# The found indices turned and copied directly behind the gathers, ahead of the projections and their evacuation

## The reference

```python
sim = jnp.where(jnp.arange(Tn) <= i, k @ q_i, -jnp.inf)
_, top_idx = jax.lax.top_k(sim, M)               # M = 8 keys out of at most 256
idx = jnp.concatenate([jnp.full((nc, 1), i), top_idx[slots]], axis=1)
K = k[idx]; V = v[idx]                            # subsets of 2 and of 3 keys
det = jnp.linalg.det(jnp.einsum('cnd,cmd->cnm', K, K))
score = log(where(valid, det, 1.0) + 1e-06) / (s + 1)
out_s = softmax(K @ q_i / 4) @ V                  # per subset
y = softmax(scores) @ outs
```

## Time and profile before

| what | value |
|---|---|
| median of 3 runs | 6865.02 us (6857.94 to 6873.23) |
| profiled execution | 6853.56 us |
| its span | 6851.9 us |
| PE busy in the span | 4985.4 us (73%) |
| DVE busy | 4293.3 us (63%) |
| POOL busy | 3267.7 us (48%) |
| ACT busy | 2061.2 us (30%) |
| mean granted TensorE clock | 0.731 |

### The profile page before, as it was taken

One profiled execution on the slowest core, in us unless ns is written; L12 is line 12 of the kernel. 1 busy time (PEld: TensorE's weight loads), 2 busy tenths in 40 slices (PEclk: granted clock), 3 DMA queues, 4 the chain that ended last, 5 costly groups with the idle time before them and its releaser, 6 DMA issues. The chain is left out here.

```text
span 6851.9 us, 140450 instructions
## 1 busy us (share of the span) xinstructions
PE 4985.4 (73%) x45364; PEld 3654.2 (53%) x45365; DVE 4293.3 (63%) x9002; ACT 2061.2 (30%) x6098; POOL 3267.7 (48%) x4341
## 2 busy tenths in 40 slices
PE   5777776987878888888888888334971997169990
PEld 2333333775555555555555555333850776069990
DVE  5777776227889989999899999723654333212223
ACT  3343333223333333333333333221210332123330
POOL 1222222115667777777777777334235000554447
PEclk8676777997666666666666666557985996589995
DMA  4000000002222222222222222212222002111113
GB/s 140 7 5 5 7 3 6 0 4 73 74 73 75 75 73 76 73 76 75 75 76 73 76 76 74 57 37 72 76 72 60 0 0 61 56 50 45 46 43 110
DMA packets 170739, 369.46 MB, mean 54 GB/s; under 512 B 35650, under 2 KB 100939, under 8 KB 169140
## 3 DMA queue, kind: packets, MB, share of 16 engines
q1 hardware_dynamic: 136404, 283.77, 12.6%
q0 software_dynamic: 33792, 78.69, 3.6%
HBM read 286.86 MB, written 75.50 MB: 53 GB/s over the span
## 5 line engine op out<-in xcount | busy, mean ns | idle before, releaser
L2333 POOL TENSOR_TENSOR l2a_prod<-l2a_keys 128x64 f32<-128x64 f32 (+1 forms) x2304 | 1143.7, 528 | 626.9 <-ACT l2a_norms L2224 619.7
L2678 PE MATMUL l2a_g<-l2a_feat,l2a_onehot 128*128 128x33 bf16 x27648 | 828.3, 187 | 49.4 <-DVE l2a_onehot L2544 24.8
L2678 PEld LDWEIGHTS l2a_g<-l2a_feat,l2a_onehot 128*128 128x128 bf16 x27648 | 807.2, 103 | 57.5 <-DVE l2a_onehot L2544 32.3
L2647 PE MATMUL l2a_s<-l2a_qkT 32*128 32x128 f32 (+1 forms) x1536 | 612.9, 489 | 53.3 <-issue 53.2
L2544 DVE TENSOR_SCALAR l2a_onehot<-l2a_spread,l2a_key_col 128x2048 bf16<-128x2048 bf16 x576 | 545.7, 974 | 141.4 <-DMA l2a_spread<-index_rows 105.1
L1734 POOL TENSOR_TENSOR l_hc<-l_hs,l_bc 128x512 f32<-128x512 f32 x192 | 243.1, 1266 | 794.2 <-DVE l_hs L1808 790.7
L2553 DVE TENSOR_REDUCE l2a_dots<-l2a_prod 128x72 f32<-128x1152 f32 x384 | 515.7, 1343 | 54.2 <-POOL l2a_prod L2339 54.2
L1903 PE MATMUL l_y<-l_hc,l_selT 128*96 128x512 f32 x384 | 308.2, 897 | 294.0 <-POOL l_hc L1734 294.0
L2596 PE MATMUL l2a_a<-l2a_tT,l2a_wqk 96*96 96x256 f32 x1024 | 408.9, 570 | 124.5 <-ACT l2a_tT L2175 124.5
L2222 ACT COPY l2a_keys<-l2a_g 128x128 f32<-128x128 f32 x768 | 199.7, 260 | 816.5 <-PE l2a_g L2678 800.5
L440 POOL DMA_INDIRECT rows_in<-l3f_dispatch_xn,l3f_dispatch_at x128 | 122.9, 960 | 652.5 <-ACT l3f_dispatch_xn L416 613.8
(11 more groups left out here) (403 smaller groups left out, 10979.3 us busy)
## 6 DMA issues: line engine op xcount, KB each, us to landing
l2a_spread<-index_rows SPq DMA_DIRECT2D x384, 512.0 KB, 3.7
rows_in<-main_zeros SPq DMA_DIRECT2D x1, 13824.0 KB, 59.4
l2f_xg<-rows_in SPq DMA_DIRECT2D x72, 192.0 KB, 2.4
rows_out<-l2f_ys POOLq DMA_DIRECT2D x72, 192.0 KB, 2.4
l3f_xg<-rows_in SPq DMA_DIRECT2D x72, 192.0 KB, 2.4
rows_out<-l3f_ys POOLq DMA_DIRECT2D x72, 192.0 KB, 2.4
l3f_w<-in_l3f_w SPq DMA_DIRECT2D x2, 4608.0 KB, 33.9
l_xT<-in_l_xT SPq DMA_DIRECT2D x16, 384.0 KB, 3.8
```

Source lines behind the costliest of these rows:

```text
L2333: nc.gpsimd.tensor_tensor(made[:, j, at:at + wide * wide, :].rearrange("p (b a) f -> p b a f", b=wide), key[:, lo:lo + wide, :].unsqueeze( ...
L2647: nc.tensor.matmul(o, qkT[rows, u, h // 3, t * P:(t + 1) * P], qkT[rows, u, 4 + h // 3, 0:nk], start=True, stop=False, skip_group_check=True)
L2678: ins = nc.tensor.matmul(g_ps[j][:, a * FEAT:(a + 1) * FEAT], onehot[:, s[2] % 2, kt, j * SLOTS + a, :], feat3[:, s[1], kt, piece, h, :], ...
```

## The change

On ACT `copy_turned` moves from the end of the body to the place right behind `cast_index`, ahead of the stage functions, `normalise` and the evacuation of `front`. On PE `turn_index` moves from the end of the body to the place right behind the gathers, ahead of `turn_output` and `front`. All instructions, waits and buffers stay the same.

```diff
@@ ACT
                     if real:
                         cast_index(n, u, i)
+                        copy_turned(n, u, i)
                     for k, do in ((SIMS, differences), (DENOM, denominators), (GAP, gaps), (DET, logs),
                                   (SCORE, weights), (OUT, out)):
...
                     if i == 0 and real:
                         split_middle(n, u)
-                    if real:
-                        copy_turned(n, u, i)
@@ PE
                     if s3:
                         gather(s3, 0)
                         gather(s3, 1)
+                    if not (isinstance(n, int) and n == B):
+                        turn_index(n, u, i)
                     if previous(n, u, i, OUT):
                         turn_output(*previous(n, u, i, OUT))
                     nxt = next_image(n, u, last)
                     if nxt and FRONT <= i < FRONT + 8:
                         front(*nxt, i - FRONT)
-                    if not (isinstance(n, int) and n == B):
-                        turn_index(n, u, i)
```

## The result

The changed kernel takes **7087.14 us** (median of 4 runs, 7079.75 to 7122.75), the kernel before 6863.94 (4 runs, 6857.94 to 6873.23). The ratio is 1.0334 with an interval of [1.0298, 1.0371]: 3.3% slower, where +22 us and a range up to 6960 had been forecast. The profiled execution took 7079.75 us, its span 7078.1 against 6851.9, its mean granted clock 0.694 against 0.731.

The account below looks back on a forecast made before the run. DVE was taken as the bound at 90% busy, PE close behind at 82%. A PE loss of 88 us less a gain of 66 us gave +22 us on 6865, so 6887 us, range 6805 to 6960.

Parts of the forecast that it names:

- The spread waits go: DVE's one-hot comparison (L2544): its waits for the spread indices, 105.1 us, nearly vanish, to under 20 us.
- The gain of 66 us: DVE in steps 2 and 3: earlier indices save 2.13 us per image, limited by POOL's product, over 31 images.
- ACT's wait for PE, costed at nothing: ACT's early copy waits for PE's turn, 0.6 us per step with the copy, covered by later waits for DVE.
- The order on PE, 74 us: PE, steps 3 to 10: turn ahead of front work delays the gather of step 11, 2.4 us per image over 31.
- The clock, 14 us: PE's granted clock: added pauses cost a quarter of one front's 1.76 us, 0.44 us per image.
- Rival 3: PE's clock: one to two more fronts per image at the low level, 80 us more, 6967 us; chance 0.15.
- What would show it: Signs in the changed profile's attention stage: waits, PE pauses, step 11's gather 2 to 4 us later, DVE busy 2507 us.

Follow-up runs that it names:

- e3: Kernel before with the copy of the turned indices early on ACT only in steps 11, 0, 1 and 2, PE unchanged: 6829.19 us, ratio 0.9945.
- e1: Kernel before with only ACT's part, the copy directly behind the cast in all steps, PE unchanged: 6864.91 us, ratio 0.9992.
- e5: e3 plus eight small unread matmuls behind the gathers in every step, the turn still last: 6792.23 us, ratio 0.9879.
- e11: e4 again with more runs, the changed kernel with eight small matmuls ahead of each turn: 6873.96 us, ratio 1.0009.
- e4: Changed kernel with eight small unread matmuls ahead of each turn: 6889.65 us in one run, 1.0036 of the kernel before.
- e6: e4 with four small matmuls before every turn in place of eight: 6997.48 us in one run, ratio 1.0174.
- e9: Kernel before with eight small unread matmuls behind the gathers in every step, nothing else: 6812.4 us, ratio 0.9917.

## Why the prediction was wrong

The sign was right; the size was not (+223 us by the medians, against +22), and the true value lies beyond the range. Step by step:

- **The spread waits go.** Right: 105.1 to 11.0 us. The copy starts 0.47 us after its cast's end in the mean, 1.15 us at most.
- **The gain of 66 us.** Too large: 38 us (e3). What failed there is "POOL's product, issued at 2795.52 and 0.74 us long": the duration is that of a product with no one-hot beside it. With about 1.15 us in both steps the 1.88 us become 1.88 − 0.8 = 1.1 us, and 31 images make 34 us; from the mean of 2.13 us it is 41 us. e3 gave 38. The one-hots show the same: a pair takes 4.62 us beside POOL's weighing (2945.59 and 2946.09, above) and 1.39 us where POOL idles (2964.49). The weighing ends at 2949.67 and the pair 0.54 us later, at 2950.21. So it goes throughout: in the changed kernel's trace 329 of the 576 one-hots start while a POOL instruction runs, and each ends at least 0.547 us after that instruction does, 0.55 in the median, though one alone takes 0.74 us in all. In these rows one engine stands while the other works. The Trainium skill ("SBUF — State Buffer", "Who interferes with whom") has GpSimd and DVE share a port pair that one of them holds for its whole instruction while the other is blocked; these rows agree. This is read from traces, and no run took the two engines apart.
- **ACT's wait for PE, costed at nothing.** Not refuted for the changed kernel: with the turn early ACT waits 0.44 us before its copy. With the turn late it is dear: e1 is 36 us above e3. In steps 3 to 10 the two edits belong together, or neither.
- **The order on PE, 74 us.** The mechanism holds, and the size is near at a high clock: 89 us (e5 to e11). Part of that is luck. Measured as in the last point below, the gather of step 11 ends 4.2 us later in e11 than in e5 (59.3 against 55.1 us), where the sum had 2.4; only 2.9 us per image, 89 over 31, reached the time. The pause of 0.69 us stands before the turn in steps 6 to 11, front behind it, as foretold. The claim that there is little cover was sound for most of it: the waits of L2552 rose well past 100 us.
- **The clock, 14 us.** This is the step that failed and that made the error: "I take a quarter of one front, 0.44 us, per image". By the experiments it is about 178 us, 5.7 us per image, or more than three fronts' worth of 1.76 us. Two things were wrong in it. It priced only the front, while all of PE's work hangs on the level: the scores grew by 102 us, the projections L2595 by 63 us, all of PE by 240 us over the span (5225.6 against 4985.4) with the same 45364 instructions. And it took the long waits for what lowers the level and counted their shortening in the change's favour. The long wait of the projections did vanish (124.5 to 0.7 us), PE's idle time in pauses over 2 us fell from 323 to 234 us, its whole idle time did not grow, and the level still fell. That added matmuls bring it back is a run's result (e4, e6, e11). That the many short pauses are what lowered it fits the rows, but is argued: e6 has less idle time of PE in the stage than e11 (370 us against 420) and as few pauses over 0.5 us (142 against 166), and its level is 0.63, not 0.76. And in the kernel before PE worked 16 us without a pause at 0.50. What sets the level stays open. The Trainium skill ("TensorE: Matmul & The Clock Gate", Part 1) has the throttled clock as the default that activity releases. The runs agree: by that rule eight useless matmuls per step should speed up even the unchanged kernel, and e9 did by 0.8%. How far one single pause moves the level was not tried.
- **Rival 3** had the mechanism, with +80 us on top of the forecast. It was given 0.15 because the longest idle times get shorter, the same misjudgement.
- **What would show it.** The gather of step 11 was to end 2 to 4 us later against DVE's step 3; from the end of L2427 to the end of that gather it is 64.6 us in the image above (2913.55 to 2978.14), and over 31 images, worked out in the same way, 64.6 us in the mean against 56.8 before: 7.7 us. DVE's busy time, forecast unchanged at 2507, is 2599; of these 92 us 58 are one-hots, which stood more behind long POOL instructions (52 took over 1.5 us before, 113 us in all; 61 after, 181 us). The level moved by 0.08, beyond the 0.03 that the text named as proof against it.

## What to carry to other kernels

In a queue that runs in order, a short wait moved ahead of independent work costs its round trip in every step, and on a nearly full PE it can cost more through the clock than through the wait: here about 178 us against 89. Price a change in PE's pauses over all of PE's work at both levels, not over the instructions next to the pause. The sum of the idle time did not show the danger here; the number of pauses did, though it did not predict the level of e6. If one product must be had early, move it only in the steps that have no cover to lose (e3), and try a few matmuls whose result nobody reads behind the gathers (e5: 6792 us, 1.2% below the kernel before).

## What the hardware showed that was not expected

- PE busy 92% of 42.5 us at a level of 0.50, with a pause of 0.69 us (once 1.34 us) in each step; before, PE busy without a pause for 16 us at 0.50. Four added matmuls per step gave a stage level of 0.63, eight 0.75 to 0.76, against 0.58 with none.
- 3072 extra matmuls (128x16 by 128 columns, bf16, 300.9 us of PE time in e11) made the kernel before 0.8% and the changed one 3.1% faster.
- POOL's product of 128x256 elements went from 0.74 to 1.19 us, and DVE's one-hot pair from 1.39 to 4.62 us, where both engines had work: one stood until the other's instruction ended.
